# A gated linear recurrence beside a ternary feed-forward: roots, products and scans in PSUM, and the output projection on split parts

## The chip, the cores and the metric

The kernel runs on one core of a Trainium2 chip. Its engines each work off a list of instructions of their own and meet at semaphores: TensorE (matrix products, which it writes to PSUM, eight banks of 512 f32 columns), VectorE, ScalarE (functions from tables, copies), GpSimd, and SyncE, which issues DMAs. The metric is the device time of one execution in microseconds; lower is better.

## The reference

```python
xn = layernorm(x)                                   # x: 2 sequences of 512 tokens, 256 wide
# recurrent branch
y    = gelu(xn @ w_y + b_y)
xb   = xn @ w_x + b_x
conv = conv_b + sum(conv_w[k] * shifted(xb, k))     # 4 taps over time
gate_x = sigmoid(conv @ w_ig + b_ig)
gate_a = sigmoid(conv @ w_ag + b_ag)
log_a  = -8 * gate_a * softplus(a_param)
a      = exp(log_a)                                 # 0 at the first token
mult   = sqrt(1 - exp(2 * log_a))                   # 1 at the first token
h      = scan(h = a * h + gate_x * conv * mult)     # over the 512 tokens
attn   = (h * y) @ w_out + b_out
# feed-forward branch, w1, w3, w2 rounded to (-s, 0, s)
g      = silu(xn @ w1q.T) * (xn @ w3q.T)            # 682 wide
out    = x + attn + g @ w2q.T
```

All data is f32.

## The kernel before

Channels lie on the 128 partitions and tokens along the free dimension, except for x and the output, where tokens lie on the partitions. There are two sequences s, each of 512 tokens; 256 channels are two chunks c of 128; the hidden width 682 is five full blocks j of 128 and a tail of 42. A unit of elementwise work is 128x512.

TensorE's f32 products are made in split parts where they are many: an operand v is cut into v_hi, which is v rounded to the type fp32r, and v_lo = v - v_hi, and w·v is taken as w_hi·v_hi + w_lo·v_hi + w_hi·v_lo. v_hi is a copy, mostly by ScalarE; v_lo is a subtraction, mostly by GpSimd. The ternary weights are exact in fp32r, so there v_hi and v_lo are two terms. The output projection alone takes its operands whole: f32 h·y against f32 w_out (L706), 16 matmuls in the code.

Every engine's order is written out by hand, and every dependence is a wait on a named semaphore. The part of the program at which the change works is the last third:

- TensorE runs the ten hidden blocks (`hidden(n)`, two products each into the halves of one slot; n = 0 to 4 are sequence 0, 5 to 9 sequence 1), then `down(0)` and `down(1)` (g_hi and g_lo of five blocks, the tail and b_out, accumulated in the output banks), then `project(0)` and `project(1)` onto the same banks.
- ScalarE takes SiLU of each hidden block (`silu_of`, L332), copies g to g_hi (`g_hi_of`, L338), and at the end loads the table of the square root and makes the four roots of 1 - a² (`mult_of`, L370), named for s and c.
- VectorE makes g from SiLU and the second product (`g_of`, L514), the hi and lo parts of the tail's g, and then four rounds, one for each s and c: the product of the gated input with the root (`gated_products`, L533), the scan (`scan`, L538) and the product h·y (`gated_output`, L544). Last it adds the output banks to x in five pieces (`output`, L551): two of sequence 0 and three of sequence 1, of 2, 2, 2, 1 and 1 tiles of 128 tokens.
- GpSimd makes g_lo (`lo_of_g`, L256). g and SiLU live in rings of three, so `g_of(n)` waits for g_lo of n - 3.
- SyncE issues a store for each of the five output pieces (L208) and waits for them all.

The rounds' tiles tx (gated input, then h, then h·y), ta (a) and mult (a², then its root) lie in SBUF. The names in the profile are those of buffers: w_raw is what silu and g alias, xn_y is y, slot is PSUM. A trace's "f32" of 128x1022 is two rows of 511.

Of the kernel before, what the change touches and what calls it, by code (L numbers as in the profile page):

```python
# [43 lines left out]
def build(nc: bass.Bass, x, dense, w13t, w2t, params, b_out, out):  # L44
# [7 lines left out]
    with ctx:  # L52
# [128 lines left out]
        def _(sp):  # L181
# [31 lines left out]
        def _(pool):  # L213
# [62 lines left out]

        @block.scalar
        def _(act):
# [138 lines left out]
            for n in range(FULL, 2 * FULL):  # L417
# [3 lines left out]
            g_hi_of(2 * FULL - 1)  # L421
            for s in range(SEQS):
                for c in range(KC):
                    mult_of(s, c)
# [3 lines left out]
        def _(dve):  # L428
            nc.vector.memset(quarter[:, :], 0.25).then_inc(quarter_set, 1)
            nc.vector.memset(mult[:, :, :, 0:1], 0.5).then_inc(mult0_set, 1)  # L430
# [414 lines left out]
```

## Time and profile before

| | us |
|---|---|
| median of 3 runs | 75.66 (75.23 to 76.0) |
| profiled execution | 75.99 |
| its span | 74.20 |
| TensorE matmul busy | 69.2 (93% of the span) |
| VectorE busy | 61.2 (82%) |
| ScalarE busy | 48.3 (65%) |
| GpSimd busy | 31.5 (43%) |

The span is the stretch from the first to the last instruction of the trace; the execution's own time is 1.79 us longer. The profile tells each engine's busy time, the chain of work that ended last (followed back from the last instruction through what released each step), who waited for whom, and every instruction in order of time. A matmul's end is modelled, and neighbouring matmuls overlap, so their starts tell the pace. TensorE's granted clock was at its full level, 2.4 GHz, over the last 20 us.

### The profile page before, as it was taken

Reading aid. Unit: us, or ns where it says so; the run is one execution under the profiler, and the core shown is the slowest. Engines: PE = TensorE matmul, PEld = TensorE weight load, DVE = VectorE, ACT = ScalarE, POOL = GpSimd, SP = SyncE. Lnnn points to the kernel's source line nnn. Section 1 sums busy time; section 2 is a strip of 40 time slices with the busy share of each in tenths; the row PEclk is TensorE's granted clock in tenths of the full one; section 3 lists DMA queues with packets and bytes.
Section 4 is the critical chain, followed back from the end, with each engine's and each line's share of the span. In section 5 each row is a group of like instructions: output and inputs, shape, how many; then the busy total and the mean of one; then the engine's idle time right before and its main releaser. Section 6 shows DMA issues by size and latency. Waiting matters only on the chain.

```text
span 74.2 us, 1064 instructions
## 1 busy us (share of the span) xinstructions
PE 69.2 (93%) x364; PEld 58.6 (79%) x364; DVE 61.2 (82%) x101; ACT 48.3 (65%) x75; POOL 31.5 (43%) x43
## 2 busy tenths in 40 slices
PE   4999969999999999999999999999999999999920
PEld 4985758877888888888888888888899999988800
DVE  4897499999999999999979974697960799999750
ACT  3674523899999999999998978466699910000000
POOL 6385647245851680016002979947689000000000
PEclk9999999999999999999999999999999999999999
DMA  0889999920000000000000000000000000000195
GB/s 8 236 289 333 368 379 342 379 97 9 0 0 0 4 0 0 0 0 0 4 1 0 0 9 0 0 0 0 0 0 0 0 0 0 9 0 0 61 322 183
DMA packets 5095, 5.63 MB, mean 76 GB/s; under 512 B 525, under 2 KB 4578, under 8 KB 5090
## 3 DMA queue, kind: packets, MB, share of 16 engines
q1 hardware_dynamic: 4946, 5.55, 22.1%
q8 instruction: 3, 0.05, 0.3%
q10 hardware_dynamic: 144, 0.01, 0.1%
q14 instruction: 2, 0.02, 0.1%
HBM read 4.51 MB, written 1.05 MB: 75 GB/s over the span
## 4 chain that ended last, share of the span: by engine, by line
PE 80%; DMA 7%; DVE 5%; SPq 3%; issue 1%; DVEq 0%
PE slot L664 25%; PE slot L647 23%; PE slot L696 14%; PE slot L706 8%; DMA x_sb<-x 7%; PE slot L767 4%; PE slot L673 2%; SPq L186 2%; DVE stats L436 2%; PE slot L740 2%; DVE x_sb L551 1%; PE slot L636 1%; DVE xt_lo L455 1%; SPq L183 1%; DVEq L52 0%
## 5 line engine op out<-in xcount | busy, mean ns | idle before, releaser
L256 POOL TENSOR_TENSOR g_lo<-w_raw,g_hi 128x512 fp32r<-128x512 f32 x10 | 14.1, 1421 | 9.0 <-ACT g_hi L338 8.9
L664 PE MATMUL slot<-xt_hi,w_q 128*128 128x512 f32 x40 | 15.7, 393 | 0.0
L664 PE MATMUL slot<-xt_lo,w_q 128*128 128x512 f32 x40 | 15.7, 393 | 0.0
L514 DVE SCALAR_TENSOR_TENSOR w_raw<-w_raw,s,slot 128x512 f32<-128x512 f32 x10 | 7.3, 747 | 3.1 <-ACT w_raw L332 3.0
L696 PE MATMUL slot<-w_q,g_hi 128*128 128x256 f32 x40 | 9.7, 283 | 0.0
L696 PE MATMUL slot<-w_q,g_lo 128*128 128x256 f32 x40 | 9.7, 283 | 0.0
L492 DVE SCALAR_TENSOR_TENSOR conv<-slot,par,conv 128x511 f32<-128x511 f32 (+2 forms) x12 | 9.0, 748 | 0.4
L664 PEld LDWEIGHTS slot<-xt_hi,w_q 128*128 128x128 f32 x40 | 7.5, 188 | 1.7
L664 PEld LDWEIGHTS slot<-xt_lo,w_q 128*128 128x128 f32 x40 | 7.5, 188 | 1.7
L332 ACT ACTIVATE w_raw<-slot,scale 128x512 f32<-128x512 f32 x10 | 6.6, 684 | 3.1 <-PE slot L664 3.1
L696 PEld LDWEIGHTS slot<-w_q,g_lo 128*128 128x128 f32 x40 | 7.7, 192 | 0.0
L696 PEld LDWEIGHTS slot<-w_q,g_hi 128*128 128x128 f32 x40 | 7.7, 192 | 0.0
L226 POOL TENSOR_TENSOR w_lo<-w_raw,w_hi 128x512 fp32r<-128x512 f32 x4 | 5.2, 1295 | 4.5 <-ACT w_hi L283 3.7
L706 PE MATMUL slot<-w_raw,tx 128*128 128x256 f32 x32 | 7.1, 379 | 0.0
L338 ACT ACTIVATE g_hi<-w_raw 128x512 fp32r<-128x512 f32 x10 | 6.3, 629 | 1.1 <-DVE w_raw L514 0.9
L251 POOL TENSOR_TENSOR conv_lo<-conv,conv_hi 128x512 fp32r<-128x512 f32 x4 | 5.4, 1354 | 3.3 <-ACT conv_hi L342 3.3
L706 PEld LDWEIGHTS slot<-w_raw,tx 128*128 128x128 f32 x32 | 6.0, 190 | 0.8
L713 PE MATMUL slot<-ones 128*128 128x128 f32 x28 | 5.3, 357 | 1.0 <-POOL ones L214 1.0
L713 PEld LDWEIGHTS slot<-ones 128*128 128x128 f32 x28 | 4.8, 261 | 1.4 <-POOL ones L214 1.0
L533 DVE TENSOR_TENSOR tx<-tx,mult 128x512 f32<-128x512 f32 x4 | 2.7, 685 | 2.8 <-ACT mult L370 2.8
L538 DVE TENSOR_TENSOR_SCAN tx<-ta,tx 128x512 f32<-128x512 f32 x4 | 4.9, 1224 | 0.1
L647 PE MATMUL slot<-conv_hi,w_hi 128*128 128x512 f32 x12 | 4.7, 395 | 0.0
(111 smaller groups left out, 144.5 us busy)
## 6 DMA issues: line engine op xcount, KB each, us to landing
w_raw<-w13t SPq DMA_DIRECT2D x2, 682.0 KB, 7.6
w_raw<-dense SPq DMA_DIRECT2D x5, 256.0 KB, 5.6
out<-x_sb SPq DMA_DIRECT2D x3, 256.0 KB, 2.2
w_raw<-w2t SPq DMA_DIRECT2D x1, 640.0 KB
x_sb<-x SPq DMA_DIRECT2D x4, 128.0 KB, 2.3
x_sb<-x SPq DMA_DIRECT2D x1, 512.0 KB, 5.3
out<-x_sb SPq DMA_DIRECT2D x2, 128.0 KB, 2.1
w_raw<-w2t SPq DMA_DIRECT2D x2, 42.0 KB
```

The lines of the kernel that those rows point to most:

```text
L226: nc.gpsimd.tensor_tensor(w_lo[:, m], w_raw[:, m], w_hi[:, m].bitcast(f32), ALU.subtract).then_inc(w_lo_set, 1)
L251: nc.gpsimd.tensor_tensor(conv_lo[:, s, c], conv[:, s, c], conv_hi[:, s, c].bitcast(f32), ALU.subtract).then_inc(conv_lo_set, 1)
L256: nc.gpsimd.tensor_tensor(g_lo[:, j, s], g[:, n % RING], g_hi[:, j, s].bitcast(f32), ALU.subtract).then_inc(g_lo_set, 1)
L332: nc.scalar.activation(silu[:, n % RING], slot[H_SLOT[s][j]][:, 0], ACT.Silu, scale=scale[:, 0:1]).then_inc(silu_set, 1)
L338: nc.scalar.activation(g_hi[:, j, s], g[:, n % RING], ACT.Copy).then_inc(g_hi_set, 1)
L492: nc.vector.scalar_tensor_tensor(out=conv[:, s, c, i:], in0=slot[X_SLOT[s]][:, c, 0:SEQ - i], scalar=par[:, CONV_W + KC * k + c:CONV_W + K ...
L514: nc.vector.scalar_tensor_tensor(out=g[:, n % RING], in0=silu[:, n % RING], scalar=s32[:, 0:1], in1=slot[H_SLOT[s][j]][:, 1], op0=ALU.mult ...
L647: mm = nc.tensor.matmul(dst[:, o], w[:, m, c, o * P:(o + 1) * P], v[:, c], start=(first and i == 0 and c == 0), stop=(last and i == len(te ...
L664: mm = nc.tensor.matmul(slot[H_SLOT[s][j]][:, o], w13_q[:, c, col:col + P], v[:, s, c], start=(c == 0 and v is xt_hi), stop=(c == KC - 1 a ...
L696: nc.tensor.matmul(out_tile(s, i, t), v[:, s, rows], w2_q[:, j], start=(j == 0 and t == tiles.start and k == 0), stop=False, skip_group_ch ...
L706: mm = nc.tensor.matmul(out_tile(s, i, t), tx[:, s, c, t * P:(t + 1) * P], w_raw[:, WOUT, c], start=False, stop=(c == KC - 1), skip_group_ ...
L713: nc.tensor.matmul(slot[WARM_SLOT][:, 0, 0:P], ones[:, :], ones[:, :], start=True, stop=True)
```

## The change

- The four roots are written to three PSUM banks that nothing else uses by then (slot 1's second half, and both halves of slot 2), the fourth root to the first of them again. Product and scan work in place there; h·y reads h from PSUM and writes tx in SBUF. The first column of each bank, which was set once for all in SBUF at the start, is set by a memset for each root (`first_root`).
- h·y is cut into hy_hi (ScalarE, `hy_hi_of`) and hy_lo (GpSimd) in the tiles of conv's parts, w_out into w_hi and w_lo (both on GpSimd, between the squares of a and the first g_lo), and both calls of `project` take three fp32r terms: 48 matmuls.
- g_hi of the last g is made by GpSimd, in front of its g_lo; ScalarE takes g_hi(8) before the last SiLU.
- The fourth of the five stores is issued from ScalarE's queue.

```diff
+        hy_hi, hy_lo = conv_hi, conv_lo
...
+        S_BANK = (slot[1][:, 1], slot[2][:, 0], slot[2][:, 1])
+        def state(s, c):
+            return S_BANK[(KC * s + c) % len(S_BANK)]
...
+        def store(queue, n):
+            s, i = O_ALL[n]
+            queue.wait_ge(o_set, n + 1)
+            t = slice(O_TILES[s][i].start, O_TILES[s][i].stop)
+            queue.dma_start(out_dram[s][:, t], x_sb[:, s, t]).then_inc(out_stored, 16)
...
-            for n, (s, i) in enumerate(O_ALL):
-                sp.wait_ge(o_set, n + 1)
-                t = slice(O_TILES[s][i].start, O_TILES[s][i].stop)
-                sp.dma_start(out_dram[s][:, t], x_sb[:, s, t]).then_inc(out_stored, 16)
+            for n in (0, 1, 2, 4):
+                store(sp, n)
...
+            pool.wait_ge(a2_set, SEQS)
+            square_hi(WOUT)
+            square_lo(WOUT)
             for n in range(2 * FULL):
+                if n == 2 * FULL - 1:
+                    pool.wait_ge(g_set, n + 1)
+                    nc.gpsimd.tensor_copy(g_hi[:, HJ[n][1], HJ[n][0]], g[:, n % RING]).then_inc(g_hi_set, 1)
                 lo_of_g(n)
+            for s in range(SEQS):
+                for c in range(KC):
+                    pool.wait_ge(hy_hi_set, KC * s + c + 1)
+                    nc.gpsimd.tensor_tensor(hy_lo[:, s, c], tx[:, s, c], hy_hi[:, s, c].bitcast(f32), ALU.subtract).then_inc(hy_lo_set, 1)
...
-                nc.scalar.activation(mult[:, s, c, 1:], mult[:, s, c, 1:], ACT.Sqrt, scale=-0.25, bias=quarter[:, 0:1]).then_inc(mult_set, 1)
+                act.wait_ge(mult0_set, KC * s + c + 1)
+                nc.scalar.activation(state(s, c)[:, 1:], mult[:, s, c, 1:], ACT.Sqrt, scale=-0.25, bias=quarter[:, 0:1]).then_inc(mult_set, 1)
+            def hy_hi_of(s, c):
+                act.wait_ge(hy_set, KC * s + c + 1)
+                act.wait_ge(ga_psum, s + 1)
+                nc.scalar.activation(hy_hi[:, s, c], tx[:, s, c], ACT.Copy).then_inc(hy_hi_set, 1)
...
-                nc.vector.tensor_tensor(tx[:, s, c], tx[:, s, c], mult[:, s, c], ALU.mult).then_inc(nx_set, 1)
+                nc.vector.tensor_tensor(state(s, c), tx[:, s, c], state(s, c), ALU.mult).then_inc(nx_set, 1)
...
-                nc.vector.tensor_tensor_scan(tx[:, s, c], ta[:, s, c], tx[:, s, c], 0.0, ALU.mult, ALU.add).then_inc(h_set, 1)
+                nc.vector.tensor_tensor_scan(state(s, c), ta[:, s, c], state(s, c), 0.0, ALU.mult, ALU.add).then_inc(h_set, 1)
...
-                nc.vector.tensor_tensor(tx[:, s, c], tx[:, s, c], y[:, s, c], ALU.mult).then_inc(hy_set, 1)
+                nc.vector.tensor_tensor(tx[:, s, c], state(s, c), y[:, s, c], ALU.mult).then_inc(hy_set, 1)
...
                     gated_output(s, c)
+                    if KC * s + c == 0:
+                        dve.wait_ge(hy_set, 1)
+                        first_root(1, 1)
...
-                pe.wait_ge(w_loaded[WOUT], 16)
+                pe.wait_ge(w_lo_set, WOUT + 1)
                 for c in range(KC):
-                    pe.wait_ge(hy_set, KC * s + c + 1)
-                    for i, tiles in enumerate(O_TILES[s]):
-                        for t in tiles:
-                            mm = nc.tensor.matmul(out_tile(s, i, t), tx[:, s, c, t * P:(t + 1) * P], w_raw[:, WOUT, c],
+                    for k, (v, w, ready) in enumerate(((hy_hi, w_hi, hy_hi_set), (hy_hi, w_lo, hy_hi_set), (hy_lo, w_hi, hy_lo_set))):
+                        pe.wait_ge(ready, KC * s + c + 1)
+                        for i, tiles in enumerate(O_TILES[s]):
+                            for t in tiles:
+                                mm = nc.tensor.matmul(out_tile(s, i, t), v[:, s, c, t * P:(t + 1) * P], w[:, WOUT, c],
```

What stands on ScalarE from the SiLU of n = 7 (L332; L338 is the copy to g_hi) to the end, before:

```order
L332 ACTIVATE w_raw<-slot,scale 128x512
L338 ACTIVATE g_hi<-w_raw 128x512
L332 ACTIVATE w_raw<-slot,scale 128x512
L338 ACTIVATE g_hi<-w_raw 128x512
L332 ACTIVATE w_raw<-slot,scale 128x512
L338 ACTIVATE g_hi<-w_raw 128x512 x2
L370 ACT_TABLE_LOAD
L370 ACTIVATE mult<-mult,quarter 128x511 x4
```

and now (L359 is the SiLU, L365 the copy to g_hi, L398 the roots, L404 the copy to hy_hi, which lies in conv_hi):

```order
L359 ACTIVATE w_raw<-slot,scale 128x512
L365 ACTIVATE g_hi<-w_raw 128x512
L359 ACTIVATE w_raw<-slot,scale 128x512
L365 ACTIVATE g_hi<-w_raw 128x512 x2
L359 ACTIVATE w_raw<-slot,scale 128x512
L398 ACT_TABLE_LOAD
L398 ACTIVATE slot<-mult,quarter 128x511 x3
L404 ACTIVATE conv_hi<-tx 128x512
L398 ACTIVATE slot<-mult,quarter 128x511
L404 ACTIVATE conv_hi<-tx 128x512 x3
L190 DMA out<-x_sb 128x256
```

The last SiLU has moved behind the copy of g(8), the copy of the last g is gone, and the four copies of h·y and a store stand at the end.

VectorE from the low part of the tail's g (L572) to the third round, before:

```order
L572 TENSOR_TENSOR gt<-w_raw,gt_hi 42x1024
L514 SCALAR_TENSOR_TENSOR w_raw<-w_raw,s,slot 128x512 x2
L533 TENSOR_TENSOR tx<-tx,mult 128x512
L538 SCALAR_TENSOR_TENSOR tx<-ta,tx 128x512
L544 TENSOR_TENSOR tx<-tx,xn_y 128x512
L533 TENSOR_TENSOR tx<-tx,mult 128x512
L538 SCALAR_TENSOR_TENSOR tx<-ta,tx 128x512
L544 TENSOR_TENSOR tx<-tx,xn_y 128x512
L533 TENSOR_TENSOR tx<-tx,mult 128x512
```

and now (L554 is g, L570 the memset of a first column, L576, L581 and L587 the three steps of a round):

```order
L615 TENSOR_TENSOR gt<-w_raw,gt_hi 42x1024
L554 SCALAR_TENSOR_TENSOR w_raw<-w_raw,s,slot 128x512
L570 MEMSET slot 128x1
L554 SCALAR_TENSOR_TENSOR w_raw<-w_raw,s,slot 128x512
L570 MEMSET slot 128x1 x2
L576 TENSOR_TENSOR slot<-tx,slot 128x512
L581 SCALAR_TENSOR_TENSOR slot<-ta,slot 128x512
L587 TENSOR_TENSOR tx<-slot,xn_y 128x512
L570 MEMSET slot 128x1
L576 TENSOR_TENSOR slot<-tx,slot 128x512
L581 SCALAR_TENSOR_TENSOR slot<-ta,slot 128x512
L587 TENSOR_TENSOR tx<-slot,xn_y 128x512
```

Three memsets stand around the last g, and one between the first two rounds, which waits for the first h·y.

GpSimd from conv's low parts to the end, before:

```order
L251 TENSOR_TENSOR conv_lo<-conv,conv_hi 128x512 x4
L272 TENSOR_TENSOR b_split<-b_row,b_split 1x256
L256 TENSOR_TENSOR g_lo<-w_raw,g_hi 128x512 x10
L52 UNCONDITIONAL_BRANCH
```

and now (L239 and L243 split w_out, L296 is the last g_hi, L301 the low part of h·y, which lies in conv_lo):

```order
L268 TENSOR_TENSOR conv_lo<-conv,conv_hi 128x512 x4
L289 TENSOR_TENSOR b_split<-b_row,b_split 1x256
L239 CAST w_hi<-w_raw 128x512
L243 TENSOR_TENSOR w_lo<-w_raw,w_hi 128x512
L273 TENSOR_TENSOR g_lo<-w_raw,g_hi 128x512 x9
L296 CAST g_hi<-w_raw 128x512
L273 TENSOR_TENSOR g_lo<-w_raw,g_hi 128x512
L301 TENSOR_TENSOR conv_lo<-tx,conv_hi 128x512 x4
```

The split of w_out stands in front of all g_lo, and the four low parts of h·y behind them.

## Rows read from the trace of the kernel before

**Rows 1.** The chain of work that ended last: start us, us, what.

```profile
53.53 10.56 PE slot L696 x88
64.08 6.06 PE slot L706 x28
```

**Rows 2.** TensorE in order of time: start us, length us, line, operation, tiles.

```profile
53.37 0.28 PE L696 MATMUL slot<-w_q,g_hi 128*128 128x256 f32 x1
...
63.92 0.38 PE L706 MATMUL slot<-w_raw,tx 128*128 128x256 f32 x1
...
70.61 0.38 PE L706 MATMUL slot<-w_raw,tx 128*128 128x256 f32 x1
```

**Rows 3.** VectorE in order of time, the last g and the four rounds.

```profile
53.56 1.48 DVE L514 SCALAR_TENSOR_TENSOR w_raw<-w_raw,s,slot 128x512 f32<-128x512 f32 x2
57.87 0.69 DVE L533 TENSOR_TENSOR tx<-tx,mult 128x512 f32<-128x512 f32 x1 [2.83 <-ACT mult L370]
58.60 1.22 DVE L538 TENSOR_TENSOR_SCAN tx<-ta,tx 128x512 f32<-128x512 f32 x1
59.92 0.69 DVE L544 TENSOR_TENSOR tx<-tx,xn_y 128x512 f32<-128x512 f32 x1
60.53 0.68 DVE L533 TENSOR_TENSOR tx<-tx,mult 128x512 f32<-128x512 f32 x1
...
67.89 0.69 DVE L544 TENSOR_TENSOR tx<-tx,xn_y 128x512 f32<-128x512 f32 x1
...
70.17 0.69 DVE L551 TENSOR_TENSOR x_sb<-slot,x_sb 128x512 f32<-128x512 f32 x1 [0.39 <-PE slot L706]
...
71.11 0.41 DVE L551 TENSOR_TENSOR x_sb<-slot,x_sb 128x256 f32<-128x256 f32 x1
```

**Rows 4.** ScalarE in order of time, before the rounds.

```profile
53.57 0.69 ACT L332 ACTIVATE w_raw<-slot,scale 128x512 f32<-128x512 f32 x1 [0.64 <-PE slot L664]
54.34 0.63 ACT L338 ACTIVATE g_hi<-w_raw 128x512 fp32r<-128x512 f32 x1
...
55.72 1.28 ACT L370 ACT_TABLE_LOAD   x1
57.02 0.72 ACT L370 ACTIVATE mult<-mult,quarter 128x511 f32<-128x511 f32 x1
```

**Rows 5.** GpSimd in order of time, the ninth g_lo.

```profile
55.05 1.29 POOL L256 TENSOR_TENSOR g_lo<-w_raw,g_hi 128x512 fp32r<-128x512 f32 x1 [0.36 <-ACT g_hi L338]
```

**Rows 6.** VectorE, GpSimd and TensorE in order of time, where they meet.

```profile
36.08 2.34 DVE L526 TENSOR_TENSOR mult<-ta 128x1022 f32<-128x1022 f32 x2
...
40.14 1.22 DVE L520 SCALAR_TENSOR_TENSOR tx<-tx,conv 128x1024 f32<-128x1024 f32 x1
...
40.31 2.20 POOL L256 TENSOR_TENSOR g_lo<-w_raw,g_hi 128x512 fp32r<-128x512 f32 x1 [5.77 <-ACT g_hi L338]
...
42.72 1.41 DVE L514 SCALAR_TENSOR_TENSOR w_raw<-w_raw,s,slot 128x512 f32<-128x512 f32 x2
...
44.13 0.39 PE L664 MATMUL slot<-xt_hi,w_q 128*128 128x512 f32 x1
...
44.21 3.94 POOL L256 TENSOR_TENSOR g_lo<-w_raw,g_hi 128x512 fp32r<-128x512 f32 x3 [0.46 <-ACT g_hi L338]
...
51.16 1.29 POOL L256 TENSOR_TENSOR g_lo<-w_raw,g_hi 128x512 fp32r<-128x512 f32 x1 [0.55 <-ACT g_hi L338]
...
51.37 2.15 DVE L572 TENSOR_TENSOR gt<-w_raw,gt_hi 42x1024 fp32r<-42x1024 f32 x1
```

**Rows 7.** Groups by line and shape: count, busy us, mean ns.

```profile
L514 DVE SCALAR_TENSOR_TENSOR w_raw<-w_raw,s,slot 128x512 f32<-128x512 f32 x10 | 7.3, 747 | 3.1 <-ACT w_raw L332 3.0
...
L288 ACT ACTIVATE xt_hi<-slot 128x512 fp32r<-128x512 f32 x4 | 2.3, 596 | 1.5 <-PE slot L636 1.5
...
L430 DVE MEMSET mult<- 128x4 f32 x1 | 0.1, 62 | 0.0
```

**Rows 8.** SyncE's queue in order of time, the last two stores.

```profile
71.30 0.99 SPq L208 DMA_DIRECT2D out<-x_sb  x2
```

More of the change, by code:

```diff
@@ L172, in build @@
             sem("t_psum"), sem("silu_t_set"), sem("g_t_set"), sem("gt_hi_set"), sem("gt_lo_set"))
+        hy_hi_set, hy_lo_set = sem("hy_hi_set"), sem("hy_lo_set")
         o_psum, o_set = sem("o_psum"), sem("o_set")
         HJ = [(s, j) for s in range(SEQS) for j in range(FULL)]
+        def store(queue, n):
[3 more added lines that the diff above has]
+            queue.dma_start(out_dram[s][:, t], x_sb[:, s, t]).then_inc(out_stored, 16)
         block = ctx.enter_context(nc.Block())
@@ L222, in _, with square_hi @@
             nc.gpsimd.memset(abs_sum[:, 3:4], 0.0).then_inc(consts_set, 1)
+            def square_hi(m):
+                pool.wait_ge(w_loaded[m], 16)
+                nc.gpsimd.tensor_copy(w_hi[:, m], w_raw[:, m]).then_inc(w_hi_set, 1)
             def square_lo(m):
@@ L416, in _ @@
             g_hi_of(4)
-            for n in range(FULL, 2 * FULL):
+            for n in range(FULL, 2 * FULL - 1):
                 silu_of(n)
@@ L420, in _ @@
                     g_hi_of(n - 1)
[L421 to L424, printed above, removed]
+            g_hi_of(2 * FULL - 2)
+            silu_of(2 * FULL - 1)
+            mult_of(0, 0)
+            mult_of(0, 1)
+            mult_of(1, 0)
+            hy_hi_of(0, 0)
+            mult_of(1, 1)
+            hy_hi_of(0, 1)
+            hy_hi_of(1, 0)
+            hy_hi_of(1, 1)
+            store(act, 3)
         @block.vector
@@ L429, in _ @@
             nc.vector.memset(quarter[:, :], 0.25).then_inc(quarter_set, 1)
-            nc.vector.memset(mult[:, :, :, 0:1], 0.5).then_inc(mult0_set, 1)
             nc.vector.memset(gt[32:HALF].bitcast(f32), 1.0).then_inc(gt_pads_set, 1)
@@ L618, in _ @@
             g_of(8)
+            dve.wait_ge(g_set, 9)
+            first_root(0, 0)
             g_of(9)
+            dve.wait_ge(g_set, 10)
+            first_root(0, 1)
+            first_root(1, 0)
             for s in range(SEQS):
@@ L699, in project @@
             def project(s):
-                pe.wait_ge(w_loaded[WOUT], 16)
+                pe.wait_ge(w_lo_set, WOUT + 1)
                 for c in range(KC):
-                    pe.wait_ge(hy_set, KC * s + c + 1)
-                    for i, tiles in enumerate(O_TILES[s]):
-                        for t in tiles:
-                            mm = nc.tensor.matmul(out_tile(s, i, t), tx[:, s, c, t * P:(t + 1) * P], w_raw[:, WOUT, c],
-                                                  start=False, stop=(c == KC - 1), skip_group_check=True)
-                        if c == KC - 1:
-                            mm.then_inc(o_psum, 1)
+                    for k, (v, w, ready) in enumerate(((hy_hi, w_hi, hy_hi_set), (hy_hi, w_lo, hy_hi_set), (hy_lo, w_hi, hy_lo_set))):
[3 more added lines that the diff above has]
+                                mm = nc.tensor.matmul(out_tile(s, i, t), v[:, s, c, t * P:(t + 1) * P], w[:, WOUT, c],
+                                                      start=False, stop=(c == KC - 1 and k == 2), skip_group_check=True)
+                            if c == KC - 1 and k == 2:
+                                mm.then_inc(o_psum, 1)
             def warm(count):
```

3 lines of the change are left out of this document (2 added, 1 removed).

## The prediction

> **What bounds the kernel now.** I read the chain of work that ended last first, because it tells whose end is the end. It runs through TensorE alone from 53.53 us: the down projection to 64.08, then the output projection (L706), and last VectorE's outputs from 70.17 [rows 1, 3]. To see what stands just behind that chain I looked at both engines in order of time. Its first L706 record starts at 63.92 and its 32nd at 70.61 [rows 2]: 0.216 us apart. Sixteen f32 matmuls in the code give 32 records, so one f32 matmul costs 0.43 us, and the last chunk's eight records start at about 69.1. VectorE makes the product h·y that this chunk needs in four rounds of product, scan and gated output, the first from 57.87, the last ending at 67.89 + 0.69 = 68.58 [rows 3]. So TensorE leads VectorE by only some 0.5 us here (69.1 less 68.58). That is all that a cheaper projection can gain by itself, and anything put between h·y and TensorE above 0.5 us comes out at the end.
>
> **The change, part by part.**
>
> *Projection in split parts.* 16 f32 matmuls of 0.43 us (6.9 us) become 48 f32r ones. The down projection issues 88 matmuls of the same 128x256 shape in 10.56 us, 0.12 us each [rows 1], so 48 take 5.76 us and TensorE's own work shrinks by 1.15 us. If nothing else waited, it would end at 64.0 + 5.8 = 69.8 instead of 70.99.
>
> *The parts of h·y.* The last projection matmuls now need the low part, which is made in three steps after h·y. ScalarE's copy: 0.63 us, as that of g (54.34), which began 0.03 us after VectorE had ended g at 54.31 [rows 3, 4]. GpSimd's subtraction: 1.29 us, beginning 0.08 us after ScalarE's end (54.97 to 55.05) [rows 4, 5]. From GpSimd to TensorE no row shows the step; VectorE answers within 0.03 to 0.13 us in these rows (ScalarE's root ends at 57.74, the product starts at 57.87), and I take 0.07. Then two low-part matmuls for the first output tile pair, one behind the other (0.12 us) and the second's 0.28 us [rows 2], and 0.04 us to VectorE. Sum from the end of h·y to the first output of sequence 1: 0.03 + 0.63 + 0.08 + 1.29 + 0.07 + 0.40 + 0.04 = 2.54 us. The three earlier chunks cost nothing: each low part is ready about 2.1 us after its h·y, at about 62.6, 65.4 and 68.1, while TensorE wants them at about 65.0, 66.4 and 67.9, and the third's 0.2 us go under in the longer wait for the last chunk. The high-part matmuls of the last chunk (8 x 0.12) fit into the 1.4 us in which GpSimd makes the low part.
>
> *ScalarE's order.* The last of the copies to g_hi (L338) leaves ScalarE, but the last SiLU now stands behind g_hi(8): from 53.57 it moves to about 54.88 (g_hi(8) ends at 54.97, and neighbours overlap by some 0.09), ends at 55.57, and the table load starts there, 0.14 us before the 55.72 of now [rows 4]. VectorE's last g slides from 54.3 to 55.6, and is still done at 56.35, before the first root ends. So the first product starts 0.14 us earlier.
>
> *The last g on GpSimd.* A copy of unknown price and the subtraction behind it end by 56.4 + 1.3 + 1.3 = 59.0 at the dearest; TensorE reaches that block at about 62.6. The first low part of h·y is wanted from 61.2. Nothing.
>
> *Roots, products and scans in PSUM.* Twelve VectorE operations and four roots change where they read or write. The trace has no product, scan or root into PSUM. Bounds by the nearest rows: an operation with a PSUM source and a per-partition scalar (L514) takes 747 ns where the product from SBUF takes 690, 0.06 more [rows 3, 7]; ScalarE reading PSUM takes 596 ns where it takes 630 from SBUF, 0.03 less [rows 4, 7]. Twelve times 0.06 is +0.7 us; sixteen times -0.03 is -0.5 us. I take nought, because the nearest row of the same operation, tensor_tensor with one PSUM source, took 0.69 us [rows 3], the same as the product in SBUF. The Trainium skill, "VectorE: DVE Perf Modes", section on the TRN2 errata, gives a fixed part of 58 cycles from SBUF and 120 from PSUM; by that table the twelve operations would grow by 12 x 65 ns = 0.78 us in all. The 0.69 us row speaks against it.
>
> *Where the sources lie also decides who blocks whom.* VectorE's subtraction from two SBUF sources (L572, started at 51.37) lasted 2.15 us and ended 1.07 us after GpSimd's at 51.16 had; GpSimd's g_lo at 40.31 lasted 2.20 instead of 1.29, behind gated_input (40.14 to 41.36) [rows 6]. Two g products with one PSUM source ran at 42.72 beside GpSimd in 1.41 us, undisturbed [rows 6]. So the new operations with one PSUM source run free of GpSimd's four low parts, which then keep their 1.29 us. The Trainium skill, "SBUF — State Buffer", section "Who interferes with whom", states this as an exclusive lock of a shared port; the trace agrees (1.07 after the other's end).
>
> *The rewritten first columns.* Three memsets at 62 ns [rows 7] fall in VectorE's wait for the root. The fourth, in front of the second product, waits for h·y: 0.03 + 0.06, and the overlap of 0.08 between gated output and next product (60.61 against 60.53) is lost: +0.17 us on the chain.
>
> *Split of w_out on GpSimd.* It starts when the squares are done, at 36.08 + 2.34 = 38.42 [rows 6]. The copy's price lies between the 0.63 us of ScalarE's [rows 4] and the 1.29 of GpSimd's subtraction; since it reads one source I take 0.8, which ends the split at about 40.6. That holds gated_input(1) back by 0.5 us, and g(2) from 43.5 to 44.0. TensorE's sixth hidden block, which needs it, starts at 44.13 [rows 6]: just covered. On GpSimd a delay of 0.5 us meets an idle 0.46 us before 44.21, so the later g_lo keep their times. If the copy takes 1.29 us, TensorE waits some 0.4 us once, and that is covered at the end, where TensorE now waits for VectorE.
>
> *Outputs.* VectorE's last output ends at 71.53, but its store is second in a back-to-back pair on SyncE (71.30, 0.99 us for two) and begins only at 71.80 [rows 8]. With the fourth store on ScalarE's queue, the last is issued at once: -0.27 us, or nothing if the queues take turns.
>
> **The sum.** h·y ends at 68.58 - 0.14 + 0.17 = 68.61. The first output of sequence 1 starts at 68.61 + 2.54 = 71.15 instead of 70.17: +0.98. Less 0.27: +0.71 us. The profiled run took 75.99 us (span 74.20), 0.33 above the median of 75.66; on the median the sum gives **76.4 us**, 0.9% more. A difference under 1% counts here as no change, so the forecast lies at that line.
>
> **Rivals.**
> *A. VectorE's round is longer in PSUM* (a fixed part of 0.06 us in each of twelve). The L514 row is for it, the 0.69 us row against. 0.71 + 0.7: 77.1 us. The table of the Trainium skill's errata section, cited above, asks for the same; by it the time would be 77.2 us.
> *B. VectorE's round is shorter in PSUM*, by 0.03 us or more in each step: 0.71 - 0.5: 75.9 us; at twice that it is 75.4.
> *C. The order at the port turns over: faster than before.* VectorE's L572 lost 1.07 us to a GpSimd subtraction that began 0.2 us ahead of it (51.16, 51.37). If the delay from the w_out split passes the 0.46 us of idle by more than 0.2 us (a copy above some 1.1 us), GpSimd comes second, g(8) is early by about 1 us, and with it g_hi(8), the last SiLU, the table load and every round. Then h·y ends at 67.6, TensorE's own 5.8 us bind again, the first output starts at about 70.15, and only the store's 0.27 us is left as the difference: 75.4 us, with B's shorter rounds not much less.
> *D. The PSUM source does not keep VectorE clear of GpSimd.* Then three of the four low parts collide with a round, at up to 1.2 us each: up to 80 us. The 1.41 us row is against it.
>
> **Chances.** Forecast 0.48 (75.9 to 76.9), A 0.17, B 0.19, C 0.13, D 0.03. 75.1 to 77.3 leaves out D and the far ends of B and C. Faster by over 1% (under 74.9) needs B and C together: 0.10. Within 1%: half of the forecast, B, most of C: 0.46. Slower by over 1%: the other half, A, D: 0.44.
>
> **What would show it.** TensorE waits over 1 us in all in front of the last chunk, first for ScalarE's, then for GpSimd's part. The chain that ended last goes through product, scan and gated output, ScalarE, GpSimd and a few matmuls. The gated output of the last chunk ends at about 68.6, GpSimd's last subtraction takes 1.29. Product, scan and gated output are 0.69, 1.22 and 0.69 us. The last store is issued within 0.05 us of VectorE's end. I am wrong if the first product starts away from 57.7, if the round is not 2.66 us, or if TensorE has no wait in the projection.

## The result, and the profile after

| | changed kernel | kernel before, same comparison |
|---|---|---|
| median | 76.75 us (76.21 to 77.0, 4 runs) | 75.58 us (75.23 to 76.0, 4 runs) |
| ratio | 1.0171, 95% interval 1.0119 to 1.0223 | |
| profiled execution | 77.00 us | 75.99 us |
| its span | 74.9 us | 74.2 us |

The change makes the kernel 1.7% slower. The forecast was 76.4 us in a range of 75.1 to 77.3. The measured 76.75 lies as far from the forecast as from rival A (77.1), so the time alone does not tell them apart; the rows below do. Two sums must be kept apart: the span grew, and so did what lies outside it (median over all runs 2.04 us, before 1.80).

Positions in two traces are compared below by their distance to the first record of the output projection, because everything ahead of it shifts a little from one execution to the next (it starts at 63.92 us before [rows 2], at 63.61 now). Some executions are disturbed and run 1 to 2% longer: the medians and ratios of the experiments leave them out, and of silu_first, silu_first_whole and two_idle_semaphores, whose profiled execution was such a one, only these distances are used.

The page of the changed kernel, its first and fourth part (busy time and share of the span; the chain that ended last, by engine):

```profile
PE 69.0 (92%) x380; PEld 59.5 (79%) x380; DVE 61.8 (82%) x104; ACT 50.0 (67%) x78; POOL 39.3 (52%) x50
...
PE 53%; DVE 19%; DMA 7%; issue 6%; ACT 5%; SPq 3%; POOLq 2%; POOL 2%; DVEq 1%; ACTq 0%
```

TensorE's busy time is no shorter than before (69.2). In the last third the chain now takes in VectorE, ScalarE and GpSimd. Its end, start us, length us, what:

```profile
64.94 0.70 DVE tx L587
65.64 0.02 issue
65.67 0.64 ACT conv_hi L404
66.31 0.07 issue
66.38 1.28 POOL conv_lo L301
67.66 1.34 issue
69.00 1.33 POOLq L52
70.33 0.04 issue
70.37 0.52 PE slot L758 x2
70.90 0.02 issue
70.92 0.69 DVE x_sb L594
```

It passes from VectorE to ScalarE to GpSimd to TensorE, where before it stayed on TensorE [rows 1]. It goes by the third low part; the fourth lies right behind it, as the engines' own rows show. VectorE of the changed kernel in order of time (answers to [rows 3]; L576, L581 and L587 are product, scan and h·y, L594 the outputs):

```profile
57.34 0.70 DVE L576 TENSOR_TENSOR slot<-tx,slot 128x512 f32<-128x512 f32 x1 [1.18 <-ACT slot L398]
58.08 1.23 DVE L581 TENSOR_TENSOR_SCAN slot<-ta,slot 128x512 f32<-128x512 f32 x1
59.41 0.69 DVE L587 TENSOR_TENSOR tx<-slot,xn_y 128x512 f32<-128x512 f32 x1
60.17 0.06 DVE L570 MEMSET slot<- 128x1 f32 x1
60.21 0.70 DVE L576 TENSOR_TENSOR slot<-tx,slot 128x512 f32<-128x512 f32 x1
...
67.60 0.69 DVE L587 TENSOR_TENSOR tx<-slot,xn_y 128x512 f32<-128x512 f32 x1
...
70.92 1.35 DVE L594 TENSOR_TENSOR x_sb<-slot,x_sb 128x512 f32<-128x512 f32 x3 [1.43 <-PE slot L758]
```

The three steps take 0.70, 1.23 and 0.69 us from and to PSUM, where they took 0.69, 1.22 and 0.69 in SBUF. The last h·y ends at 68.29, 4.68 us behind the projection's start (before: 68.58, 4.66 behind). But the first output of sequence 1 starts 7.31 us behind it instead of 6.25: VectorE waits 1.43 us. What fills them, first ScalarE, then GpSimd of the same kernel (answer to [rows 4, 5]):

```profile
68.33 0.63 ACT L404 ACTIVATE conv_hi<-tx 128x512 fp32r<-128x512 f32 x1 [2.03 <-DVE tx L587]
71.97 0.35 ACTq L190 DMA_DIRECT2D out<-x_sb  x1
```

```profile
38.20 0.61 POOL L239 CAST w_hi<-w_raw 128x512 fp32r<-128x512 f32 x1 [3.95 <-DVE mult L566]
38.89 1.29 POOL L243 TENSOR_TENSOR w_lo<-w_raw,w_hi 128x512 fp32r<-128x512 f32 x1
...
69.04 1.28 POOL L301 TENSOR_TENSOR conv_lo<-tx,conv_hi 128x512 fp32r<-128x512 f32 x1 [1.38 <-ACT conv_hi L404]
```

And TensorE (answers to [rows 2]):

```profile
63.61 0.64 PE L758 MATMUL slot<-w_hi,conv_hi 128*128 128x256 f32 x4
...
66.99 0.64 PE L758 MATMUL slot<-w_lo,conv_hi 128*128 128x256 f32 x4
67.71 0.74 PE L758 MATMUL slot<-w_hi,conv_lo 128*128 128x256 f32 x4
69.01 0.74 PE L758 MATMUL slot<-w_hi,conv_hi 128*128 128x256 f32 x4 [0.56 <-ACT conv_hi L404]
69.59 0.63 PE L758 MATMUL slot<-w_lo,conv_hi 128*128 128x256 f32 x4
70.37 0.74 PE L758 MATMUL slot<-w_hi,conv_lo 128*128 128x256 f32 x4
```

The four starts of a group of four are 0.12 us apart, so its real work ends about 0.5 us after its start. TensorE waits some 0.2 us for the third low part (67.5 to 67.71), is through with three chunks at about 68.2, then stands for 0.8 us until ScalarE's part is there (69.01), works 1.0 us and stands again until GpSimd's is (70.37).

The end of the kernel, SyncE's stores in order of time and its waits (total us, times, longest) of the changed kernel:

```profile
68.92 3.73 SPq L190 DMA_DIRECT2D out<-x_sb  x4
```

```profile
SPq L52 <- DMA out<-x_sb: 1.9, 1, 1.9
```

VectorE ends at 72.27, and the last issue ends at 72.65, 0.38 behind it; before it ended 0.76 behind (71.53, 72.29). But the wait for the data is now 1.9 us, and was 1.5.

### The profile page after: what moved, and what is told of

Same layout as the page of the kernel before. It is cut to its first block, busy times and chain, and to the rows that moved or that the text cites. A ratio compares the mean times of both kernels' runs of the same rounds, so it can differ in the third digit from the quotient of the medians.

```text
span 74.9 us, 1114 instructions
## 1 busy us (share of the span) xinstructions
PE 69.0 (92%) x380; PEld 59.5 (79%) x380; DVE 61.8 (82%) x104; ACT 50.0 (67%) x78; POOL 39.3 (52%) x50
## 4 chain that ended last, share of the span: by engine, by line
PE 53%; DVE 19%; DMA 7%; issue 6%; ACT 5%; SPq 3%; POOLq 2%; POOL 2%; DVEq 1%; ACTq 0%
PE slot L698 23%; PE slot L715 20%; DMA x_sb<-x 7%; DVE slot L581 5%; PE slot L819 4%; DVE gt L615 3%; DVE slot L576 3%; PE slot L724 2%; SPq L201 2%; DVE tx L587 2%; DVE stats L476 2%; ACT w_raw L359 2%; PE slot L792 2%; POOLq L52 2%; POOL conv_lo L301 2%
## 5 line engine op out<-in xcount | busy, mean ns | idle before, releaser
L554 DVE SCALAR_TENSOR_TENSOR w_raw<-w_raw,s,slot 128x512 f32<-128x512 f32 x10 | 7.3, 747 | 3.9 <-ACT w_raw L359 3.8
L243 POOL TENSOR_TENSOR w_lo<-w_raw,w_hi 128x512 fp32r<-128x512 f32 x5 | 6.5, 1292 | 4.6 <-ACT w_hi L310 3.7
L301 POOL TENSOR_TENSOR conv_lo<-tx,conv_hi 128x512 fp32r<-128x512 f32 x4 | 5.1, 1283 | 7.1 <-ACT conv_hi L404 7.1
L359 ACT ACTIVATE w_raw<-slot,scale 128x512 f32<-128x512 f32 x10 | 6.6, 682 | 2.3 <-PE slot L715 2.3
L404 ACT ACTIVATE conv_hi<-tx 128x512 fp32r<-128x512 f32 x4 | 2.5, 632 | 7.4 <-DVE tx L587 7.4
L365 ACT ACTIVATE g_hi<-w_raw 128x512 fp32r<-128x512 f32 x9 | 5.7, 629 | 2.6 <-DVE w_raw L554 2.5
L765 PE MATMUL slot<-ones 128*128 128x128 f32 x28 | 5.8, 403 | 1.0 <-POOL ones L227 1.0
L765 PEld LDWEIGHTS slot<-ones 128*128 128x128 f32 x28 | 5.7, 313 | 1.0 <-POOL ones L227 1.0
L581 DVE TENSOR_TENSOR_SCAN slot<-ta,slot 128x512 f32<-128x512 f32 x4 | 4.9, 1228 | 0.1
L698 PE MATMUL slot<-conv_hi,w_lo 128*128 128x512 f32 x12 | 4.7, 393 | 0.0
```

Source lines behind the costliest of these rows:

```text
L243: nc.gpsimd.tensor_tensor(w_lo[:, m], w_raw[:, m], w_hi[:, m].bitcast(f32), ALU.subtract).then_inc(w_lo_set, 1)
L301: nc.gpsimd.tensor_tensor(hy_lo[:, s, c], tx[:, s, c], hy_hi[:, s, c].bitcast(f32), ALU.subtract).then_inc(hy_lo_set, 1)
L359: nc.scalar.activation(silu[:, n % RING], slot[H_SLOT[s][j]][:, 0], ACT.Silu, scale=scale[:, 0:1]).then_inc(silu_set, 1)
L365: nc.scalar.activation(g_hi[:, j, s], g[:, n % RING], ACT.Copy).then_inc(g_hi_set, 1)
L554: nc.vector.scalar_tensor_tensor(out=g[:, n % RING], in0=silu[:, n % RING], scalar=s32[:, 0:1], in1=slot[H_SLOT[s][j]][:, 1], op0=ALU.mult ...
L581: nc.vector.tensor_tensor_scan(state(s, c), ta[:, s, c], state(s, c), 0.0, ALU.mult, ALU.add).then_inc(h_set, 1)
```

## The experiments

Distances are in us from the first record of the output projection. "Outside" is the time less the span, the median over all runs.

| kernel | ratio to before (95%) | median | first output of sequence 1 | outside |
|---|---|---|---|---|
| changed | 1.0171 (1.0119 to 1.0223) | 76.75 | 7.31 | 2.04 |
| store_on_sync | 1.0198 (1.0150 to 1.0246) | 77.00 | 7.29 | 2.01 |
| whole_projection | 1.0047 (1.0006 to 1.0087) | 75.74 | 6.25 | 2.06 |
| rounds_in_sbuf | 1.0663 (1.0602 to 1.0723) | 80.37 | 11.17 | 2.03 |
| last_chunk_whole | 1.0029 (0.9996 to 1.0061) | 75.69 | 5.90 | 1.93 |
| silu_first | 1.0025 (0.9981 to 1.0070) | 75.80 | 6.27 | 2.15 |
| silu_first_last_whole | 0.9914 (0.9867 to 0.9962) | 75.04 | 5.34 | 2.05 |
| silu_first_whole | 1.0041 (1.0003 to 1.0080) | 76.07 | 6.25 | 2.20 |
| two_idle_semaphores | 0.9976 (0.9929 to 1.0023) | 75.33 | 6.25 | 1.84 |
| last_copy_on_gpsimd | 1.0049 (0.9996 to 1.0102) | 75.97 | 6.24 | 2.03 |
| no_gpsimd_copy | 0.9886 (0.9842 to 0.9930) | 74.45 | 5.34 | 1.80 |
| after_no_gpsimd_copy | 1.0138 (1.0096 to 1.0181) | 76.77 | 7.30 | 2.05 |
| last_copy_as_product | 1.0027 (0.9969 to 1.0086) | 75.90 | 6.25 | 2.04 |

The median of the kernel before was 75.58, 75.61, 75.44 and 75.65 us in the four sets of runs. In last_copy_on_gpsimd and last_chunk_whole VectorE shows no wait ahead of this output.

### The stores

store_on_sync is the changed kernel with all five stores on SyncE again.

```diff
-            for n in (0, 1, 2, 4):
+            for n in range(len(O_ALL)):
                 store(sp, n)
...
-            store(act, 3)
```

> The changed kernel with one edit: the fourth store goes back to SyncE's queue. Theory 1 (the last stores are bound by the rate of their data, some 0.5 MB in 1.5 us behind the first of the three, not by when they are issued): the store on ScalarE's queue gave nothing, so this one stays at the changed kernel's time, 76.75 us within 0.1, though the last store is issued about 0.25 us after VectorE's end instead of 0.03. Rival (the term of the prediction: an issue 0.27 us earlier ends 0.27 us earlier): 77.0 us.

SyncE's stores, and its last wait:

```profile
69.16 4.08 SPq L190 DMA_DIRECT2D out<-x_sb  x5
```

```profile
SPq L52 <- DMA out<-x_sb: 1.5, 1, 1.5
```

By the time alone the rival has it: 77.00 us is its number. But the ratios differ by less than their intervals, so the medians can't tell a quarter of a microsecond. The traces can. The last issue comes late again and the wait is short again, and the last packet of the stores ends 10.52 us behind the projection's start, in the changed kernel 10.55 (DMA views in steps of 0.015 us). whole_projection and the kernel before, whose outputs are at the same place as each other's, are a second such pair: 9.50 us with the fourth store on ScalarE, 9.50 without. So in both pairs of traces issuing early gave nothing; that the medians of the first pair differ by 0.25 us is within their noise. What the DMAs of the changed kernel moved from 68 to 75 us, GB/s in 40 equal slices of 0.175 us:

```profile
GB/s 0 0 0 0 0 0 0 0 0 0 94 345 310 339 375 340 334 357 345 158 0 0 0 0 0 35 293 369 328 369 328 339 340 339 252 6 0 0 0 0
```

The second stretch is the last three pieces, 0.5 MB at about 340 GB/s: 1.5 us. That stretch has no gap in which a piece that is asked for sooner could be moved.

### The split of the projection

whole_projection undoes it: f32 h·y against f32 w_out, no parts of h·y or w_out; roots, products and scans stay in PSUM.

```diff
-            square_hi(WOUT)
-            square_lo(WOUT)
...
-                    for k, (v, w, ready) in enumerate(((hy_hi, w_hi, hy_hi_set), (hy_hi, w_lo, hy_hi_set), (hy_lo, w_hi, hy_lo_set))):
+                            mm = nc.tensor.matmul(out_tile(s, i, t), tx[:, s, c, t * P:(t + 1) * P], w_raw[:, WOUT, c],
...
-            hy_hi_of(0, 0)
```

> The changed kernel without the split projection: f32 h·y against f32 w_out as before, no hy_hi, hy_lo, w_out parts; roots, products and scans stay in PSUM, the last g_hi stays on GpSimd. Theory 1 (the steps ScalarE, GpSimd, TensorE behind the last h·y cost the time): TensorE binds again, first output of sequence 1 within 0.1 us of where it stood before, relative to the start of the down projection, 75.6 us. Rival (PSUM rounds, memsets or the order on ScalarE cost it): stays at 76.3 us or more.

VectorE, the last three outputs:

```profile
70.25 1.35 DVE L583 TENSOR_TENSOR x_sb<-slot,x_sb 128x512 f32<-128x512 f32 x3 [0.37 <-PE slot L746]
```

With the projection starting at 64.00 this is 6.25 us behind, what it was before the change. The whole 1.06 us belongs to the split. What is left of the slowdown (0.5%) is not in that place; 0.25 us of it is outside the span.

last_chunk_whole keeps the split for three chunks and takes only the last one whole, which needs no part behind the last h·y.

```diff
+                    if (s, c) == (SEQS - 1, KC - 1):
+                        terms = ((tx, w_raw, hy_set),)
...
-            hy_hi_of(1, 1)
```

> The changed kernel, but the last of the four chunks (sequence 1, second half of the channels) is projected whole in f32, so that no part has to be made behind the last h·y. Theory 1 (latency behind the last h·y): TensorE has the other three chunks done by then, takes the last h·y 0.05 us after it is there, and needs 1.7 us for 8 records; the first output starts about 1.5 us earlier than in the changed kernel, and the stores' data, 1 MB at about 0.34 MB per us, allow 1.3 us of it: 75.4 us. Rival (TensorE's own work or the stores' latency bind): 76.2 us or more.

TensorE, VectorE and SyncE's last wait:

```profile
68.62 1.99 PE L761 MATMUL slot<-w_raw,tx 128*128 128x256 f32 x8
```

```profile
68.48 2.66 DVE L592 TENSOR_TENSOR x_sb<-slot,x_sb 128x512 f32<-128x512 f32 x5
```

```profile
SPq L52 <- DMA out<-x_sb: 2.2, 1, 2.2
```

The path is gone, and VectorE runs all five outputs without a wait, through at 71.14: 7.26 us behind the projection's start, before 7.61. Of those 0.35 us, 0.1 arrives at the end: the last packet ends 9.41 us behind that start, before 9.50. The first store is issued where it was (69.19, before 69.21), the 1 MB moves without a gap, and the last wait is 2.2 us in place of 1.5. Outputs that come faster than the data moves, some 0.34 MB per us here, only queue. The expected 75.4 us had this rate in it and still granted 1.3 us against the changed kernel; by the last packet it was 1.14 us, by the medians 1.06.

### The rounds' place

rounds_in_sbuf is the changed kernel with roots, products and scans in SBUF.

```diff
-            return S_BANK[(KC * s + c) % len(S_BANK)]
+            return mult[:, s, c]
```

> The changed kernel with roots, products and scans in the SBUF tile mult, in the same order and with the same waits; only the memory differs. Theory 1 (two SBUF sources on VectorE and a GpSimd subtraction exclude each other for a whole instruction): three scans begin behind a low part that started just before them and lose about 1.2 us each, so the last h·y comes 3 us or more later, some 79.8 to 80.3 us. Rival (where the tiles lie does not matter, the two engines share): rounds of 2.66 us and 76.7 us.

VectorE, and GpSimd's low parts:

```profile
56.64 1.25 DVE L576 TENSOR_TENSOR mult<-tx,mult 128x512 f32<-128x512 f32 x1 [1.22 <-ACT mult L398]
...
60.78 2.27 DVE L581 TENSOR_TENSOR_SCAN mult<-ta,mult 128x512 f32<-128x512 f32 x1
...
65.82 1.50 DVE L587 TENSOR_TENSOR tx<-mult,xn_y 128x512 f32<-128x512 f32 x1
...
69.29 1.51 DVE L587 TENSOR_TENSOR tx<-mult,xn_y 128x512 f32<-128x512 f32 x1
```

```profile
60.69 1.29 POOL L301 TENSOR_TENSOR conv_lo<-tx,conv_hi 128x512 fp32r<-128x512 f32 x1 [3.35 <-ACT conv_hi L404]
64.60 2.18 POOL L301 TENSOR_TENSOR conv_lo<-tx,conv_hi 128x512 fp32r<-128x512 f32 x1 [2.62 <-ACT conv_hi L404]
68.07 2.18 POOL L301 TENSOR_TENSOR conv_lo<-tx,conv_hi 128x512 fp32r<-128x512 f32 x1 [1.29 <-ACT conv_hi L404]
```

From the first product to the end of the last h·y it is 14.16 us here and 10.95 in the changed kernel, and the difference of 3.2 is four stretched operations: 0.55, 1.04, 0.81 and 0.82. The scan at 60.78 began 0.09 us behind a low part and ended 1.07 us behind its end (61.98), and the low part at 64.60 began behind a scan and took 2.18 us in place of 1.29. The expectation had three stretched scans; it was a product (beside the last g_lo), one scan and two h·y, so its sum came out by luck. The Trainium skill, "SBUF — State Buffer", section "Who interferes with whom", describes an exclusive lock; the rows agree, on both sides. A PSUM source is what kept the changed kernel clear of it. From the end of the last h·y to the first output of sequence 1 it is 3.25 us here and 2.63 in the changed kernel. These 0.6 us are TensorE's clock: the last low part is there at 72.80, and TensorE comes to it at 73.38. (Together that is 3.8 us between the two traces, and 3.6 between the medians.) The windows of this kernel (us; busy PE, PEld, DVE, ACT, POOL with counts; granted clock; DMA share; GB/s):

```profile
57.00:64.00 7.00, 7.00 (x61) 7.00 (x60) 6.66 (x8) 2.13 (x5) 1.62 (x2) 1.00 0.01 2
64.00:69.00 5.00, 3.29 (x23) 2.70 (x23) 4.83 (x5) 1.15 (x2) 3.11 (x2) 1.00 0.00 0
70.30:71.40 1.10, 1.10 (x4) 0.92 (x4) 1.10 (x3) 0.57 (x1) 0.00 (x0) 0.50 0.00 0
71.50:74.50 3.00, 2.94 (x13) 2.63 (x12) 0.94 (x2) 0.00 (x0) 1.27 (x1) 0.50 0.53 175
```

After waits that left TensorE busy for 3.3 of 5 us, the granted clock is 0.50, that is 1.2 GHz, and groups of four matmuls stand 1.0 and 0.85 us apart (71.51, 72.53, 73.38) instead of 0.5. The same view of the changed kernel, around its waits:

```profile
66.00:69.00 3.00, 2.36 (x18) 1.95 (x16) 2.86 (x5) 0.93 (x2) 1.28 (x1) 1.00 0.00 0
69.00:72.00 3.00, 1.95 (x12) 1.54 (x12) 1.57 (x4) 0.00 (x0) 1.28 (x1) 1.00 0.51 175
```

There the waits are shorter and the clock stays at 1.00, 2.4 GHz.

### Where the lost microsecond can be had back

silu_first puts the last SiLU ahead of the copy of g(8), and both last high parts of g on GpSimd.

```diff
-                if n == 2 * FULL - 1:
+                if n >= 2 * FULL - 2:
...
-            g_hi_of(2 * FULL - 2)
             silu_of(2 * FULL - 1)
```

> The changed kernel with the last SiLU ahead of g_hi(8) again, and g_hi(8) made by GpSimd like g_hi(9): the root's table is loaded about 1.1 us earlier, when the last SiLU is done. Theory 1 (the latency behind the last h·y sets the end, and what starts the rounds earlier gives it back until TensorE binds): first product at about 56.3, last h·y at about 67.2, TensorE's last low-part matmuls follow the high-part ones with almost no wait, first output of sequence 1 at about 69.8 instead of 70.9: 75.8 us. Rival (the rounds are not what the end waits for): 76.7 us.

VectorE, the last g, the first product and the last outputs:

```profile
55.34 0.75 DVE L553 SCALAR_TENSOR_TENSOR w_raw<-w_raw,s,slot 128x512 f32<-128x512 f32 x1
...
57.55 0.69 DVE L575 TENSOR_TENSOR slot<-tx,slot 128x512 f32<-128x512 f32 x1 [1.32 <-ACT slot L398]
...
71.12 1.35 DVE L593 TENSOR_TENSOR x_sb<-slot,x_sb 128x512 f32<-128x512 f32 x3 [1.43 <-PE slot L757]
```

The last g follows the one before it at once, without the 1.14 us that VectorE waited for the SiLU in the changed kernel. With the projection at 64.85 the first product stands 7.30 us ahead of it (6.27 in the changed kernel, 6.05 before), so the rounds begin 1.03 us earlier (silu_first_last_whole, which has the same order, has 7.29), and the first output is 6.27 behind. That pays for the path and no more: the ratio is 1.0025, and the 75.8 us are those expected.

silu_first_last_whole joins this order with the whole last chunk, silu_first_whole with the whole projection; their diffs are those above.

> The same order on ScalarE and GpSimd, and the last chunk projected whole in f32. Theory 2 (the stores' data stream, 1 MB at about 0.34 MB per us from the first store on, is what kept the run with the last chunk whole at 75.8 us, though VectorE was done 0.4 us earlier than before): with the rounds 1.1 us earlier the first store goes out about 1.1 us earlier too, and the end comes 1 us earlier than before the change, 74.8 us. Rival (the time of VectorE's last output plus a fixed 2.4 us is what counts, or TensorE's pace): 75.3 us or more.

> The same order on ScalarE and GpSimd, with the whole projection in f32 as before the change: h·y comes 1.1 us earlier, but TensorE needs 6.9 us for the projection from about 64.0 on. Both theories: TensorE binds, the last output ends at about 71.5 as before the change, and only the first two stores go out earlier: 75.5 to 75.7 us. If it were 75.0 or less, the earlier first stores alone would have been enough.

Of the first, TensorE and VectorE:

```profile
68.02 1.89 PE L760 MATMUL slot<-w_raw,tx 128*128 128x256 f32 x8
```

```profile
69.08 1.35 DVE L591 TENSOR_TENSOR x_sb<-slot,x_sb 128x512 f32<-128x512 f32 x3 [0.49 <-PE slot L760]
```

The first output is 5.34 us behind the projection's start, 0.91 earlier than before the change, and the ratio 0.9914 is below 1. In silu_first_whole it is 6.25, because the f32 projection's own matmuls bind, and the early rounds are wasted. Both were expected faster than they are: 74.8 us for the first, where 75.04 was measured, and 75.5 to 75.7 for the second, where it was 76.07. The time outside the span, which no expectation of these two had in it, is 0.25 and 0.4 us longer than before. So the split projection does pay 0.9 us of the span, but only where the rounds start early and nothing is split behind the last h·y. Neither alone has it.

### The time outside the span

Of the +1.17 us between the medians, 0.24 is outside the span. Four theories were tried, and none held. First, two more semaphores than before: two_idle_semaphores adds two that nothing uses.

```diff
+        idle_a, idle_b = sem("idle_a"), sem("idle_b")
```

> The kernel before the change with two more semaphores that nothing uses, as the changed kernel has two more. In the changed kernel and all its variants the time outside the traced span was 2.0 to 2.1 us, in the kernel before 1.8. Theory S (each semaphore costs outside the span): 0.2 us more than the kernel before, 75.9 us, with 2.0 us outside the span. Rival (it comes from the order at the end or the start): no difference, 75.7 us, 1.8 us outside.

Outside: 1.84 us, where the kernel before had 1.80 in the same set. These two semaphores are not it. Second, a copy on GpSimd, which the kernel before has nowhere: last_copy_on_gpsimd gives the kernel before one of them, the last g_hi.

```diff
+                if n == 2 * FULL - 1:
+                    pool.wait_ge(g_set, n + 1)
+                    nc.gpsimd.tensor_copy(g_hi[:, HJ[n][1], HJ[n][0]], g[:, n % RING]).then_inc(g_hi_set, 1)
...
-            g_hi_of(2 * FULL - 1)
```

> The kernel before with one edit: GpSimd makes the last g_hi instead of ScalarE, and ScalarE goes straight on to the root's table. Every kernel with a copy on GpSimd spent 1.9 to 2.2 us outside the traced span, the kernel before 1.8. Theory C (a copy on GpSimd costs some 0.25 us outside the span): about 2.05 us outside. Inside, the rounds start up to 0.7 us earlier (table loaded when g_hi(8) ends, at 54.97 instead of 55.72), which changes nothing while TensorE binds. Total 75.9 us. Rival (the time outside has another source): 1.8 us outside, total 75.6 us.

It rose from 1.78 to 2.03, as the theory had it. And no_gpsimd_copy, which is silu_first_last_whole with ScalarE making the high part of w_out behind the SiLU of block 5 and the last two g_hi behind the third root, and GpSimd the low part of w_out behind all g_lo, had 1.80 again:

```diff
-            square_hi(WOUT)
-            square_lo(WOUT)
             for n in range(2 * FULL):
-                if n >= 2 * FULL - 2:
...
-                    nc.gpsimd.tensor_copy(g_hi[:, HJ[n][1], HJ[n][0]], g[:, n % RING]).then_inc(g_hi_set, 1)
                 lo_of_g(n)
+            square_lo(WOUT)
...
+                if n == FULL:
+                    square_hi(WOUT)
...
             mult_of(1, 0)
+            g_hi_of(2 * FULL - 2)
+            g_hi_of(2 * FULL - 1)
```

> The fastest version so far (last SiLU first, last chunk whole), with no copy on GpSimd: the high part of w_out is made by ScalarE behind the SiLU of n = 5, the last two g_hi by ScalarE behind the third root, the low part of w_out by GpSimd behind all g_lo. The rounds and TensorE's work stay as they are (first output of sequence 1 about 5.3 us after the projection's start). Theory C: 1.8 us outside the span and 74.9 us. Rival: 2.05 us outside and 75.2 us as before. If GpSimd's later parts come too late, TensorE waits before the second or third term and the time is longer.

It is the fastest kernel of the study, 1.1% below the one before (74.45 us, expected 74.9): the first output at 5.34 us, as in silu_first_last_whole, and 0.25 us less outside. Up to here the theory of the copy stood. Two last kernels were to confirm it. after_no_gpsimd_copy takes the two copies out of the changed kernel itself (first lines; the low part of w_out moves behind all g_lo here too); last_copy_as_product replaces the one of last_copy_on_gpsimd by a multiplication (second).

```diff
-            square_hi(WOUT)
...
-                    nc.gpsimd.tensor_copy(g_hi[:, HJ[n][1], HJ[n][0]], g[:, n % RING]).then_inc(g_hi_set, 1)
...
+                if n == FULL:
+                    square_hi(WOUT)
...
             mult_of(1, 0)
+            g_hi_of(2 * FULL - 1)
             hy_hi_of(0, 0)
```

```diff
-                    nc.gpsimd.tensor_copy(g_hi[:, HJ[n][1], HJ[n][0]], g[:, n % RING]).then_inc(g_hi_set, 1)
+                    nc.gpsimd.tensor_scalar(g_hi[:, HJ[n][1], HJ[n][0]], g[:, n % RING], 1.0, None, ALU.mult).then_inc(g_hi_set, 1)
```

> The changed kernel without its two copies on GpSimd: the high part of w_out is ScalarE's copy behind the SiLU of block 5, the copy of the last g stands on ScalarE behind the third root, and the low part of w_out stands on GpSimd behind all low parts of g. Theory C (a copy on GpSimd costs about 0.25 us outside the traced span): the path behind the last h·y is untouched, so the first output of sequence 1 still starts 7.3 us after the projection, and only the time outside the span falls from 2.04 to about 1.8 us; ratio to the kernel before about 1.014, 76.5 us where the changed one has 76.75. Rival (the time outside the span belongs to the last stores or to the queue they are issued from): it stays at 2.0 us or more, and the ratio at 1.017.

> The kernel before with the last g's high part on GpSimd, made by a tensor_scalar multiplication by 1.0 in place of the copy. GpSimd runs such multiplications in the kernel before as well, on small tiles. If it is the copy instruction that costs outside the span, the time outside goes back to about 1.8 us and the ratio to about 1.000 or a little under, where the copy gave 1.0049 and 2.03 us. Rival: any further large operation that GpSimd takes over costs there, and the time outside stays at 2.03 us.

Both refute it. Without a copy on GpSimd the changed kernel still has 2.05 us outside, and with the multiplication it is 2.04. (The ratio of the first, 1.0138, is the one that the theory asked for, but it is also within the noise of the changed kernel's 1.0171.) The rival of the first expectation, that the place of the stores sets it, doesn't fit either: no_gpsimd_copy issues its fourth store from ScalarE, as the changed kernel does, and has 1.80. That of the second, that any large operation more on GpSimd costs, fails on no_gpsimd_copy too, whose GpSimd has 47 operations where the kernel before has 43. So the 0.24 us are measured and their cause is open. What the fourteen programs show is a pattern and no cause: ScalarE has 75 or 79 operations on the page of the three with 1.80 to 1.84 us, and 73, 74, 76, 77, 78 or 80 on those of the others, which have 1.93 to 2.20. A page has many counts, and one of them may sort fourteen programs by chance; no run here varied it by itself.

## Why the prediction was right

The direction, the mechanism and most terms held. The sum had +0.71 us, and +1.17 was measured; the 0.46 us between them were missed in two places. (Against the forecast of 76.4 it is 0.35, as the kernel before came out 0.08 lower in this comparison.) The prediction put no more than 0.44 on a slowdown of over 1%, which it was.

*TensorE is only 0.5 us ahead of VectorE, and what goes between h·y and TensorE comes out at the end.* Held. The path was put at 2.54 us and measured 2.63: 0.04 to ScalarE, 0.63, 0.08, 1.28, 0.05 to TensorE and 0.55 to the first output, where 0.44 had been taken for the last. The first output of sequence 1 is late by 1.06 us (7.31 less 6.25); the sum had 0.98. Two kernels show that the path is the cause: without the split 6.25 again, and without the parts of the last chunk alone VectorE has no wait at all.

*The earlier chunks cost nothing.* Held: TensorE waits for the third low part, 0.2 us as forecast, and this goes under in the wait in front of the last chunk, 0.8 us by the starts for ScalarE's part and some 0.3 for GpSimd's. "Over 1 us in all" was right.

*ScalarE's order and the fourth memset.* Taken together +0.03 us at the last h·y; measured +0.02 (4.68 less 4.66). That it fits to 0.01 us is in part luck: the first product starts 0.22 us earlier (6.27 us ahead of the projection, before 6.05), where 0.14 was forecast, and from it to the end of the last h·y it is 0.24 us longer (10.95, before 10.71), where 0.17 was. Of these, 0.19 is the memset's: the second product starts 0.80 us after the first h·y does, before 0.61 [rows 3].

*Rounds in PSUM at nought.* Held to 0.01 us per operation. Rivals A and B fell with it, and with A the table of the Trainium skill's "VectorE: DVE Perf Modes", section on the TRN2 errata: by an estimate from it, 62 more cycles for a PSUM source would have made 0.75 us of each 0.69, and the rows show 0.69 and 0.70. B's bound was also misread: it took ScalarE's gain in reading PSUM for VectorE's operations and for the roots, which read SBUF. And "most of C" can't be within 1%: if B and C together are 0.10 of the chances, 0.03 of C's 0.13 is left.

*Split of w_out and last g on GpSimd, covered.* Held. The copy takes 0.61 us, a little under the lower bound of 0.63, so gated_input(1) was held back by 0.2 us and not 0.5, and rival C, which needed a copy above 1.1 us, did not come about.

*Rival D, no cover from a PSUM source.* Fell in the changed kernel, where all four low parts took 1.28 or 1.29 us; rounds_in_sbuf shows what the other case costs, 80.4 us, near the 80 that was put on it.

*The last store issued at once, -0.27 us.* This step failed. It was issued at once, but the prediction took the last issue for the end. The last three stores' data set the end; the wait for them grew by the 0.4 us that the issue was early, and store_on_sync, without the edit, moves its last packet 10.52 us after the projection's start, against 10.55. "Nothing if the queues take turns" was the right value, for another reason: the data's rate.

*The time outside the span*, 0.24 us, was in no term. The sum carried the 1.79 us of the kernel before over to the changed one. The experiments found that this time is a property of the program, between 1.8 and 2.2 us, but not what sets it.

With the store at nought and these 0.24 us the sum would have been 0.98 + 0.24 = 1.22 us; +1.17 was measured.

## What to carry to other kernels

Before an operand is split for a faster matmul, look how far the matmul engine is ahead of the operand's producer: the split's copy and subtraction (2 us here) are serial behind the last producer, and only the last chunk needs to be left whole to take them off the path. An edit that frees one engine pays only together with the one that feeds it: here the split with the last chunk left whole and the earlier rounds gave nothing singly (last_chunk_whole 1.0029, silu_first_whole 1.0041) and 0.9 us of the span together. At the end of a kernel, look at the stores' data and the time outside the span as well as at the issue of the last store.

## What was not expected of the hardware

The time outside the span is not a constant of the kernel's shape: it stayed within 0.22 us of its median in all runs of one program, and the medians differed by up to 0.4 us between programs that compute the same with the same stores; its cause is open. A copy from f32 to fp32r on GpSimd takes 0.61 us for 128x512, as long as ScalarE's 0.63 and less than half of GpSimd's subtraction (1.29); the multiplication by 1.0 that does the same took 1.50 in its one record, part of it beside a product of VectorE. The four stretched operations of VectorE in rounds_in_sbuf included the scan, 2.27 us for 1.23.
